# Attention inside a two-layer graph kernel: mask on VectorE, two of eight heads exponentiated straight from the scores, rows normalised two graphs at a time

## What is computed

```
x = x + gnn(layernorm(x), adj, ...)          # 8 heads of 16
    q, k, v = split_heads(x @ W + b)
    scores  = where(adj > 0, q k^T / 4, -9e15)
    out     = softmax(scores) @ v
    return out @ Wo + bo
x = x + ffn(layernorm(x), ...)               # shared expert + top 2 of 8 routed experts
```

## Time and profile before

| what | us |
|---|---|
| three timed runs | 1353.40, 1342.87, 1353.49 (median 1353.4) |
| profiled execution, its own time | 1348.24 |
| its span in the trace | 1346.4 |
| busy: TensorE, VectorE, GpSimd, ScalarE | 1087.5, 1032.0, 922.8, 837.6 |
| row maxima L474, 128 of them | 155.8 |
| subtraction L477, 128 of them | 156.8 |
| exponentials L619, 128 of them | 135.2 |
| granted TensorE clock over the span | 0.946 of full speed |

### The profile page before, as it was taken

The page is one execution under the profiler, slowest core; times in us unless marked ns, Lnnn a source line. Parts: engine busy times, 40 slices in busy tenths (PEclk is TensorE's granted clock), DMA queues, the critical chain, the costliest instruction groups (busy, mean ns, idle before and its releaser), DMA issues. The chain is left out here.

```text
span 1346.4 us, 39563 instructions
## 1 busy us (share of the span) xinstructions
PE 1087.5 (81%) x12580; PEld 783.5 (58%) x12581; DVE 1032.0 (77%) x2503; ACT 837.6 (62%) x1449; POOL 922.8 (69%) x929
## 2 busy tenths in 40 slices
PE   0788899889899988987288999799999999979200
PEld 0456666666666666665156677477777777768200
DVE  3578888888888888887467888487777777657498
ACT  0577777777777777774076788577766666567100
POOL 3336888888888888886766777457777777766300
PEclk9999999999999999999588999899999999999755
DMA  2113323333323333221334644244444444334399
GB/s 74 32 45 86 85 75 89 87 90 90 92 74 87 86 90 90 77 63 43 102 100 119 171 144 137 67 91 99 97 103 93 92 98 96 81 67 78 115 343 310
DMA packets 276548, 136.53 MB, mean 101 GB/s; under 512 B 195142, under 2 KB 254700, under 8 KB 276474
## 3 DMA queue, kind: packets, MB, share of 16 engines
q1 hardware_dynamic: 242938, 93.39, 28.7%
q0 software_dynamic: 16896, 33.86, 7.8%
q10 hardware_dynamic: 16640, 8.39, 2.1%
HBM read 47.95 MB, written 54.04 MB: 76 GB/s over the span
## 5 line engine op out<-in xcount | busy, mean ns | idle before, releaser
L1362 POOL DMA_INDIRECT pairs_dram<-x_rows x272 | 281.2, 1034 | 121.8 <-issue 81.8
L1040 ACT ACTIVATE hid<-Z,biases 128x512 f32<-128x512 f32 (+1 forms) x336 | 208.2, 632 | 141.1 <-PE Z L1008 88.7
L1055 DVE SCALAR_TENSOR_TENSOR h<-hid,h 128x512 f16<-128x512 f32 (+1 forms) x288 | 183.2, 649 | 54.3 <-ACT h L1031 49.6
L474 DVE TENSOR_REDUCE smax<-S 128x8 f32<-128x1024 f32 x128 | 155.8, 1217 | 73.7 <-PE S L730 72.2
L1020 PE MATMUL Y<-w,h 128*128 (+1 forms) x3168 | 192.8, 220 | 11.5 <-DVE h L1055 9.2
L1020 PEld LDWEIGHTS Y<-w,h 128*128 128x128 f16 x3168 | 185.6, 99 | 28.0 <-issue 10.6
L477 DVE TENSOR_TENSOR probs<-S,smax 128x1024 f32<-128x1024 f32 x128 | 156.8, 1225 | 14.4
L1153 POOL DMA_INDIRECT slots_dram<-x_rows,pair_slot x128 | 134.7, 1052 | 47.3 <-issue 27.3
L1008 PE MATMUL Z<-x_rows,w 128*128 128x512 f16 (+1 forms) x720 | 148.3, 352 | 11.3 <-DMA x_rows<-slots_dram 7.6
L619 ACT ACTIVATE probs<-probs 128x1024 f32<-128x1024 f32 x128 | 135.2, 1056 | 21.5 <-DVE probs L477 20.3
L339 POOL DMA_INDIRECT slots_dram<-x_rows,pair_slot x116 | 121.4, 1047 | 28.1 <-issue 16.8
(11 more groups left out here) (211 smaller groups left out, 2171.1 us busy)
## 6 DMA issues: line engine op xcount, KB each, us to landing
y_pairs<-pairs_dram SPq DMA_DIRECT2D x32, 512.0 KB, 5.9
x_res<-in_x_dram SPq DMA_DIRECT2D x32, 256.0 KB, 3.5
adj<-in_adj_dram SPq DMA_DIRECT2D x32, 256.0 KB, 3.2
xT_dram<-xT SPq DMA_DIRECT2D x32, 256.0 KB
xTu<-xT_dram SPq DMA_DIRECT2D x32, 256.0 KB, 2.9
out_dram<-x_res ACTq DMA_DIRECT2D x16, 512.0 KB, 7.9
pairs_dram<-x_rows POOLq DMA_INDIRECT x272
slots_dram<-x_rows,pair_slot POOLq DMA_INDIRECT x256
```

The lines of the kernel that those rows point to most:

```text
L474: dve.tensor_reduce(smax[:].rearrange("p (r e) -> p r e", e=2), S_heads, AX_X, ALU.max).then_inc(s["max_done"], 1)
L1040: act.activation(self.hid[:, c, 0:w], self.bank(b, c)[:, 0:w], ACT.Gelu, bias=bias[:, c:c + 1], scale=1.0 / (XS * WS)).then_inc(self.gelu_ ...
L1055: dve.scalar_tensor_tensor(out=self.piece(b)[:, 1, c, 0:w], in0=self.hid[:, c, 0:w], scalar=HS, in1=self.piece(b)[:, 0, c, 0:w], op0=ALU.m ...
L1362: pool.indirect_dma_start(pairs_dram, bass.IndirectOffsetOnAxis(ap=pair_of[n][:, j:j + 1], axis=0), y_sb[n % NY][:, j], None, bounds_check ...
```

## The change

- The mask moves from GpSimd to VectorE. For group g + 1 it is written at place 2 of group g, behind `normalise`. Its wait for the scores of the group before is gone, since VectorE has read them by then.
- The scores are computed with the sign turned (Q is scaled by -0.25, the mask adds +9e15), so the row maximum is a row minimum, and VectorE writes minimum minus score, for six heads only (`SHIFTED = 6`).
- ScalarE does the other two heads itself: two exponentials of 128x128 that read `S` and take the row minimum as a per-partition bias, with scale -1. They stand behind the second copy and ahead of the exponentials of the six heads. They signal `direct_done`, for which the next scores wait too.
- `normalise` runs once for two graphs, at places 0 and 2: one reciprocal of 16 columns, one product of 256. `ON` is used whole, a half for each graph of a pair.
- The ranks move from the bank `ON` to the spare columns of `OD`. The product with V at place 3 waits for `slot_terms`, the first operation of `place` on VectorE; `place` and the rank products wait no longer for `ON` and `norm_done`.

More of the change, by code:

```diff
@@ L106, in attention_phase @@
     rs2s = sb("rs2s", [P, GT])
-    smax = sb("smax", [P, H])
+    smin = sb("smin", [P, H])
     turn = sb("turn_dve", [P, 1])
-    rden = sb("rden", [P, H])
+    rden = sb("rden", [P, 2, H])
     S = ps("S", [P, 4, 512])
@@ L352, in _ @@
                 scatter(g - 5, 0, g * GT)
-            if has(g, -1):
-                mask(g + 1, (g + 1) % 2)
             if late:
@@ L457, in gather2 @@
             last.then_inc(s["aggr2"], 1)
[L459 to L464, removed]
+        def mask(g, q):
[6 more added lines that the diff above has]
+            wait(dve, "rec_done", pair + 1)
             if j == 0:
                 wait(dve, "aT_ps", g - 1)
-            dve.tensor_tensor(attn[:, q, j], ON_heads[:, :, 0:HD], rden[:].unsqueeze(2).to_broadcast([P, H, HD]),
+            dve.tensor_tensor(attn[:, q, j:j + 2].rearrange("p j h c -> p (j h) c"),
+                              ON_heads[:, :, :, 0:HD].rearrange("p j h c -> p (j h) c"),
+                              rden[:, :, :].rearrange("p j h -> p (j h)").unsqueeze(2).to_broadcast([P, 2 * H, HD]),
                               ALU.mult).then_inc(s["norm_done"], 1)
@@ L473, in softmax_shift @@
             wait(dve, "sub_done", t)
[L474 to L475 removed]
+            dve.tensor_reduce(smin[:].rearrange("p (r e) -> p r e", e=2), S_heads, AX_X, ALU.min).then_inc(s["min_done"], 1)
+            wait(dve, "min_done", t + 1)
             wait(dve, "pt_ps", 2 * (t - 1))
[L477 to L479 removed]
+            dve.tensor_tensor(probs[:, b, 0:SHIFTED].rearrange("p (r e) k -> p r e k", e=2),
+                              smin[:, 0:SHIFTED].rearrange("p (r e) -> p r e", e=2).unsqueeze(3).to_broadcast([P, SHIFTED // 2, 2, P]),
+                              S_heads[:, 0:SHIFTED // 2], ALU.subtract).then_inc(s["sub_done"], 1)
         def choose(g, q):
@@ L502, in choose, with place @@
                                      op0=ALU.mult, op1=ALU.add).then_inc(s["rest_done"], 1)
-        def place(g, q, turned):
+        def place(g, q):
             wait(dve, "rank_ps", g + 1)
-            wait(dve, "on_ps", turned)
             dve.tensor_tensor(eq[:], RANK, pick[:, q, 0:GT], ALU.mult).then_inc(s["slot_terms"], 1)
@@ L521, in step @@
                 gather1(1, 1)
+                mask(0, 0)
                 return
@@ L543, in drain @@
             a, b = NG - 2, NG - 1
-            normalise(NT - 3, b, 1, 1)
+            normalise(NT // 2 - 2, b, 1, 0)
             residual(a, LAST[a, "out"])
-            normalise(NT - 2, b, 1, 2)
             stats2(a)
             gather2(a)
-            normalise(NT - 1, b, 1, 3)
+            normalise(NT // 2 - 1, b, 1, 2)
             choose(a - 2, 0)
@@ L553, in drain @@
             gather2(b)
-            place(a - 2, 0, NT)
+            place(a - 2, 0)
             for g in range(a - 1, NG):
                 choose(g, g % 2)
-                place(g, g % 2, NT)
+                place(g, g % 2)
         pair_blocks(dve, step)
@@ L573, in evac @@
                 wait(act, "q_ps", g + 1)
-                act.activation(QT[:, q], M0[:, :], ACT.Identity, bias=qb[:], scale=0.25 / (XS * WS)).then_inc(s["q_sb"], 1)
+                act.activation(QT[:, q], M0[:, :], ACT.Identity, bias=qb[:], scale=-0.25 / (XS * WS)).then_inc(s["q_sb"], 1)
             elif task == "K":
@@ L669, in m0_task @@
             elif task == "aT":
-                wait(pe, "norm_done", (g + 1) * GT)
+                wait(pe, "norm_done", (g + 1) * GT // 2)
                 bank = last_bank(g, task)
@@ L673, in m0_task @@
                     wait(pe, "sub_done", NT)
+                    wait(pe, "direct_done", NT)
                 else:
@@ L699, in m0_task, with rank @@
                 mm.then_inc(s["lg_ps"], 1)
-        def rank(g, q, tiles):
+        def rank(g, q, copied):
             wait(pe, "pick_done", g + 1)
             wait(pe, "counted", g + 1)
-            wait(pe, "norm_done", tiles)
+            wait(pe, "o_sb", copied)
             pe.matmul(RANK, rt.before[:], pick[:, q, 0:GT], start=True, stop=False)
@@ L781, in turn_output @@
             wait(pe, "o_sb", t + 1)
-            wait(pe, "norm_done", t)
+            wait(pe, "norm_done", t // 2)
             for a in range(2):
-                mm = pe.transpose(ON[:, a * P:(a + 1) * P], oT[:, a], ident[:])
+                mm = pe.transpose(ON_turned[:, t % 2, a], oT[:, a], ident[:])
             mm.then_inc(s["on_ps"], 1)
```

9 lines of the change are left out of this document (4 added, 5 removed).

## The result

The changed kernel takes 1383.25 us (median of 4 runs, 1381.66 to 1385.38) against 1348.13 us before (4 runs, 1342.42 to 1353.49). The ratio is 1.026, with a 95% interval of 1.020 to 1.032: slower, as forecast, by 35 us where 24 to 26 were forecast. The profiled execution took 1381.66 us, its span 1379.8.

The account below looks back on a forecast made before the run. The prediction took the scores' beat as the bound, with ScalarE's new exponentials between second copy and next scores. 0.77 us a group over 31.75 groups adds 24 to 1348.2, 1372; it said 1374, range 1345 to 1395.

Parts of the forecast that it names:

- What bounds it: Scores set the beat, 18.21 us a group; the only room is four gaps after the second copy, 0.08 to 0.51 us.
- The sum: Over the attention phase: 0.77 us more per group, 31.75 groups, 24 us added to the profiled 1348.2, giving 1372.
- The size of the gap: Second copy to next scores: two exponentials of 0.355 us, less overlaps, plus the semaphore step, 0.53 us.
- the last term: Step from the semaphore to the start of the scores on TensorE, taken as 0.04 us.
- Where the second copy stands in its beat: Its end on ScalarE stays at places 1, 2 and 0 (4.22, 4.58, 3.75 us); at place 3 0.36 sooner.
- slot_terms at place 3: The product with V's new wait for VectorE lets the scores start at 4.80 us, just covered by the 4.84 beat.
- VectorE's savings: Lighter subtraction and paired normalise, less the added mask: 1.3 us less per group, all of it becoming idle time.
- the sentence on the port pair: VectorE's mask can be held by up to a GpSimd operation of 1.04 us, inside its cover.
- Faster: Rival: the exponentials do not end last, TensorE's own queue sets the beat, the gaps close, 1325 us; chance 0.09.
- No change: Rival: the direct exponentials are cheap or half hidden, 0.25 us each, +3 us, 1352 us; chance 0.16.
- The slowed choose: Rival: VectorE's small operations beside GpSimd cost up to 0.86 us each, 19 us on top, 1393 us; chance 0.09.
- The dear pair: Rival: ScalarE's direct exponentials take 0.465 us each without overlap, a gap of 0.97, +80 us; chance 0.04.

## Why the prediction was right

**What bounds it.** Right. The gap between the second copy and the next scores was the place to look at, and the four gaps after are 0.66, 0.65, 0.75 and 0.66 us instead of 0.08, 0.51, 0.21 and 0.19 (the 0.75 is 0.66 in every second group). That the pair costs through its place in the queue is shown twice over: alone it costs the whole 35 us and more, and moved ahead of the copy it turns into a gain. One reading was loose: the 0.14 us by which ScalarE was said to be ahead on the average is the sum of its waits divided by all 99 graphs, with nothing set against it where ScalarE was the later one. The sum does not use it.

**The size of the gap.** Right in kind, too small: 0.53 was forecast. The pair itself was close, 0.368 us each and 0.62 together, against 0.355 and 0.60:

```profile
L621 ACT ACTIVATE probs<-S,smin 128x128 f32<-128x128 f32 x186 | 57.8, 368 | 0.0
```

What was mis-sized is the last term, the step from the semaphore to the scores. I took the 0.04 of a single wait, and it was 0.15, since the late semaphore is the second of two waits. That is 0.11 of the 0.12 to 0.13 that the gap came out too large. The row of before could not show it, as its scores at that place had one wait; the swapped waits gave 0.09 of it back. With 19.32 us in a group instead of 18.98 the steady groups make 11 us more than was summed.

**The start.** The sum took 31.75 equal groups and put nothing down for the start of the phase. The first group lost 4 us more than the others. So the 24 became 35 roughly by three terms: 11 more by the gap, 4 more by the first group, and some 4 less behind attention. That the last two cancel is luck.

**Where the second copy stands in its beat.** At places 2 and 0 it stayed at 4.58 and 3.75, as said, and these two pay the long step in full. At place 3 it came at 4.22 (4.31 forecast). This is the long step again: the chain there starts from the exponentials, which begin 0.26 before the scores (309.81, 310.07) where 0.15 was forecast, so the copy comes 0.1 sooner and takes most of the step back. At place 1 it came at 4.09 instead of 4.22: there the first turn had waited for the exponentials before (it started 1.17 us into the beat and ended at 1.82), and no longer does (1.09 and 1.69). That small gain offset the long step, so the beat of place 1 came out at 4.75 to the digit for two wrong terms. The other beats were 5.23, 4.97 and 4.41 for 5.11, 4.84 and 4.28.

**slot_terms at place 3.** Nearly right. It was forecast as just covered at 4.80. TensorE stood 0.31 us ahead of the product with V (22 waits, 6.8 us in all), starting it 3.85 us into the beat as worked out:

```profile
313.92 0.64 PE L778 MATMUL OD<-pT,V 128*32 128x128 f32 x16 [0.31 <-DVE eq L507]
```

But the 0.96 from there to the scores was 1.12 in this group. The pair had ended at 314.81 and would have let the scores go 0.15 later; they started at 315.04, behind TensorE's own queue. So in one group of two this path was the later one, by 0.09 us, some 1.4 us over the phase. The kernel with the direct exponentials alone, which lacks this wait, has 4.88 at place 3 in both groups.

**VectorE's savings.** Right that they are idle time in this order, but for that 0.09: the subtraction took 0.954 (0.96 said), the pair of operations of `normalise` 0.251 and 0.425 (0.21 and 0.43), and the idle time ahead of the minimum grew from 30.6 us in 99 graphs to 71.7 in 93. The mask's 0.45 was right for the undisturbed one (0.42). Its mean was 0.855, and that went as the sentence on the port pair had it; the rows are below. It was covered, as the mask on GpSimd showed.

**The rivals.** *Faster* asked for a pair that does not end last, and I held that a queue served in order cannot give it. That holds for the queue as written. *No change* fell with the 0.368. *The slowed choose* fell: its operations took 0.18 to 0.24 us, with GpSimd issuing scatters beside it (304.00 and 305.40 us), as expected. Its price had a slip: 2 us against 1.48 of room is 0.5 in a group, not 0.6. *The dear pair* fell with the 0.62 for both. *GpSimd* was waited for by no other engine between 100 and 550 us, and its freed 1.94 us gained nothing.

## What to carry to other kernels

Before work is moved to an engine that looks free, find the point in that engine's queue where it will stand, and what is released behind it: 0.5 us of work for each graph on the least busy engine cost 35 us in all because it was served behind a late copy and ahead of the beat. The same work one instruction earlier, in time in which the engine waited anyway, made a kernel 57 us faster than that, and by itself gained 10 us over the kernel before. Where an instruction waits for two semaphores, it is worth trying the one that comes last first: here that gave 0.09 us at three starts of four.

## What the runs showed of the hardware

The order of two waits on TensorE's first product of the scores was worth 0.09 us: 0.15 us from the end of the last exponential to the scores with the late semaphore second, 0.06 with it first.

VectorE's mask and GpSimd's operations hold each other up. Timeline of the kernel after, two groups:

```profile
308.98 0.42 DVE L455 TENSOR_SCALAR negmask<-adj 128x512 bf16<-128x512 f32 x1
309.01 1.29 POOL L297 TENSOR_TENSOR xn<-x_res,mv 128x512 f32<-128x512 f32 x1
...
328.29 1.03 POOL L297 TENSOR_TENSOR xn<-x_res,mv 128x512 f32<-128x512 f32 x1
328.34 1.27 DVE L455 TENSOR_SCALAR negmask<-adj 128x512 bf16<-128x512 f32 x1
```

Where the mask begins 0.03 us ahead, it takes its 0.42 us and GpSimd's operation 1.29 instead of 1.03; where GpSimd begins 0.05 ahead, it takes its 1.03 and the mask 1.27. In this kernel 10 masks began 0.03 us ahead of such an operation and took 0.42, and 12 began 0.05 to 0.20 behind and took 1.12 to 1.27: the one that starts first has its normal time and the other waits. Of three masks that began only 0.02 us ahead one took 0.42, and two (347.62 and 502.16 us) took 1.34 beside a GpSimd operation of 1.03, so the order of two starts this close in the profile does not tell who waits. The Trainium skill (SBUF — State Buffer, "SBUF: two separate sides") describes this as an exclusive lock on a shared port pair, and the trace agrees. It cost nothing here: with the mask on GpSimd the time was the same.
